# One block kernel, eight PSUM banks: the attention's output product moves from the ring of four to the bank of the down product

## What is computed

```python
sa, ca, ga, sb, cb, gb = modulation(c)            # six rows of 256 per batch
h = layernorm(x) * (1 + ca) + sa
#   attention: 16 heads of 16, causal, window 128
h1 = layer_norm(h, ln1_w, ln1_b)
q, k, v = h1 @ Wq + bq, h1 @ Wk + bk, h1 @ Wv + bv
ctx = softmax(q k^T / 4 + band) @ v
y = h + ctx @ Wo + bo
y = y + gelu(layer_norm(y) @ W1 + b1) @ W2 + b2   # W1: 256 x 1024, W2: 1024 x 256
x = x + ga * y
h = layernorm(x) * (1 + cb) + sb                  # then a second feed-forward:
xr, xk = mixes of h with its row before           # r = sigmoid(xr Wr), k = relu(xk Wk)^2
out = x + gb * (r * (k @ Wv2))
```

## Time and profile before

| | us |
|---|---|
| median of 3 runs | 619.79 |
| lowest, highest | 619.2, 621.26 |
| the profiled execution, whole | 619.02 |
| its span, first to last instruction | 617.3 |
| PE busy (matrix multiplications) | 560.3 |
| PE busy (weight loads) | 436.6 |
| DVE, ACT, POOL busy | 417.1, 446.9, 378.1 |

### The profile page before, as it was taken

How to read it: one execution, slowest core, us unless ns; L and a number is a source line. 1 busy time by engine, 2 the same in 40 slices (tenths; PEclk the granted TensorE clock), 3 DMA queues, 4 the chain that set the end, 5 groups by cost and what they waited for, 6 DMA issues and landing times.

```text
span 617.3 us, 16387 instructions
## 1 busy us (share of the span) xinstructions
PE 560.3 (91%) x6448; PEld 436.6 (71%) x6448; DVE 417.1 (68%) x830; ACT 446.9 (72%) x749; POOL 378.1 (61%) x610
## 2 busy tenths in 40 slices
PE   8798987889898998999899989899999999999996
PEld 5467765666766776677667767677777768877785
DVE  4786676794656968786967777757766484465453
ACT  2616676679868787887879686978697798956642
POOL 4277527738947357676776679575748377953330
PEclk9999988989999999999999999999999999999999
DMA  5555435413224034422334152332522134111111
GB/s 163 218 162 129 115 83 161 121 53 81 74 70 111 20 86 123 102 77 71 101 96 116 43 142 88 90 91 74 135 49 69 47 87 122 55 29 36 44 44 34
DMA packets 46363, 55.72 MB, mean 90 GB/s; under 512 B 11643, under 2 KB 33469, under 8 KB 46286
## 3 DMA queue, kind: packets, MB, share of 16 engines
q1 hardware_dynamic: 44454, 53.81, 31.8%
q10 hardware_dynamic: 1832, 0.87, 0.6%
HBM read 22.31 MB, written 4.49 MB: 43 GB/s over the span
## 4 chain that ended last, share of the span: by engine, by line
PE 54%; DVE 20%; ACT 13%; issue 6%; POOL 4%; DMA 2%; ACTq 0%; SPq 0%; DVEq 0%; POOLq 0%
DVE nmax L1853 5%; PE rest L361 4%; PE rest L486 3%; PE quad L398 3%; PE rest L447 3%; PE rest L474 3%; PE rest L498 3%; PE quad L342 3%; PE rest L449 3%; PE rest L448 3%; DVE hid_lo L1914 2%; ACT p L1151 2%; PE quad L307 2%; DVE quad L1850 2%; ACT rest L1202 2%
## 5 line engine op out<-in xcount | busy, mean ns | idle before, releaser
L2588 POOL TENSOR_SCALAR_AFFINE_SELECT p<-p 128x448 f32<-128x448 f32 x64 | 39.0, 610 | 88.1 <-ACT p L1151 63.5
L1853 DVE TENSOR_REDUCE nmax<-quad 128x8 f32<-128x1032 f32 x64 | 78.9, 1233 | 2.2
L430 PE MATMUL rest<-bt_hi,w_hi 128*128 128x256 f16 x256 | 70.2, 274 | 5.0 <-DVE hid_lo L1914 3.5
L1151 ACT ACTIVATE p<-quad,scale_s 128x576 f32<-128x576 f32 (+1 forms) x73 | 59.0, 823 | 20.0 <-PE quad L342 19.7
L1202 ACT ACTIVATE rest<-rest,bias,scale_g 128x256 f32<-128x256 f32 x128 | 62.8, 533 | 12.0 <-PE rest L432 11.5
L447 PE MATMUL rest<-w_hi,hid_hi 128*128 128x256 f16 x256 | 69.9, 273 | 1.7 <-DVE hid_lo L1914 1.7
L432 PE MATMUL rest<-bt_hi,w_lo 128*128 128x256 f16 x256 | 69.8, 273 | 0.0
L431 PE MATMUL rest<-bt_lo,w_hi 128*128 128x256 f16 x256 | 69.8, 273 | 0.0
L449 PE MATMUL rest<-w_hi,hid_lo 128*128 128x256 f16 x256 | 69.8, 272 | 0.0
L448 PE MATMUL rest<-w_lo,hid_hi 128*128 128x256 f16 x256 | 69.8, 272 | 0.0
L1914 DVE SCALAR_TENSOR_TENSOR hid_lo<-rest,inv_f,hid_hi 128x512 f16<-128x512 f32 x64 | 46.5, 740 | 29.1 <-ACT hid_hi L1212 29.1
(11 more groups left out here) (239 smaller groups left out, 1544.4 us busy)
## 6 DMA issues: line engine op xcount, KB each, us to landing
k_st<-k_two SPq DMA_DIRECT2D x64, 128.0 KB, 2.5
v_blk<-vn SPq DMA_DIRECT2D x16, 512.0 KB, 6.0
q_st<-q_two SPq DMA_DIRECT2D x64, 64.0 KB, 2.2
k_st<-k_two SPq DMA_DIRECT2D x64, 64.0 KB, 2.0
rb<-den_rows SPq DMA_DIRECT2D x16, 256.0 KB
x<-x SPq DMA_DIRECT2D x16, 256.0 KB, 3.0
out<-x SPq DMA_DIRECT2D x16, 256.0 KB, 2.2
xa<-x SPq DMA_DIRECT2D x7, 512.0 KB, 4.3
```

What stands on the lines that cost most here:

```text
L430: e.matmul(dst, w1_hi[:, k, ms], bt_hi[:, k, :], start=(k == 0), stop=False)
L1151: e.activation(p32[gp % SLOTS][:, c0:c0 + 2 * w].rearrange("p (n c) -> p n c", n=2), (rest if gp < APART else quad)[:, b0 % HQ:b0 % HQ + 2 ...
L1853: e.tensor_reduce(nmax[:, :, :, qt].rearrange("p a j -> p j a"), quad[:, :, 2 * QB - 2:2 * WIN].rearrange("p j (c a) -> p j a c", a=2), AX ...
```

## The change

The output product takes its bank from `ring_f` instead of `ring_s`; `residual_a` reads it there. Its first call also waits for the last scores that lived in this bank (s_ex), and the waits in `warm` become holds, which are issued once per semaphore and value. The order of the calls stays on every engine.

```diff
             def warm(n, times):
                 if n == 0:
                     e.wait_ge(s_pool, POOL_IDENT)
-                if n == WARM:
-                    e.wait_ge(s_peak, 10)
-                if n == WARM + 5:
-                    e.wait_ge(s_ex, 2 * APART)
+                if WARM <= n < WARM + 5:
+                    hold(e, s_peak, 10)
+                if n >= WARM + 5:
+                    hold(e, s_ex, 2 * APART)
...
-                bank, free = ring_s.take(("wo", i), s_x1, i + 1)
+                bank, free = ring_f.take(("wo", i), s_x1, i + 1)
                 if t2 == 0:
                     e.wait_ge(s_ct, 2 * (n + 1))
                 if i == 0:
                     e.wait_ge(s_wos, 1)
+                    e.wait_ge(s_ex, 2 * APART)
                 hold(e, *free)
...
-                e.tensor_tensor(x1[:, ts, :], ring_s.at["wo", i][:, :].rearrange("p (t c) -> p t c", t=2), h[n % 3][:, ts, :],
+                e.tensor_tensor(x1[:, ts, :], ring_f.at["wo", i][:, :].rearrange("p (t c) -> p t c", t=2), h[n % 3][:, ts, :],
                                 ALU.add).then_inc(s_x1, 1)
```

## The result

The changed kernel is slower: 623.32 us (median of 20 runs, 620.1 to 628.51) against 619.61 us (20 runs of the kernel before, 617.24 to 622.04). The ratio is 1.0059 with a 95% interval of 1.0043 to 1.0075, that is +3.7 us (2.7 to 4.6). The forecast was 621.4 us, +1.6; the range of 617.4 to 624.4 holds the result, and slower, which the prediction counts from +1.86 us on, had its largest chance, 0.46. The range owes that to the room left for rivals 2 and 3; the sum itself is 2.1 us short.

What follows compares the result with a forecast made beforehand. PE was taken to bound most stretches, with short spells of DVE or ACT late. Gains -1.3, half batch 2 +0.3, half batch 14 +2.1 and pairs +0.5 gave +1.6 us: 621.4 us, range 617.4 to 624.4.

Steps and rivals of the forecast that it cites:

- rival 2: ACT becomes late: its 14 extra instructions cost 3.5 instead of 0.5 us; +4.6, 624.4 us, slower; chance 0.13.
- rival 3: The clock falls at PE's new pause near 553: +2.0 on top, +3.6, 623.4 us, slower; chance 0.15.
- The new wait at half batch 14: The down product, right behind the output product, waits for its bank to be read: +2.1 us, absorbed by nothing.
- Half batch 2: The down product begun at 166.85 would wait for the output product's read ending at 167.14: +0.3 us.
- The gains: Waits taken from PE at half batches 4, 6, 7, 9 and 10: -1.3 us in sum.
- Half batch 7: A 0.43 us wait goes with nothing standing behind it: -0.43 us.
- half batches 9 and 10: At 9 a 0.37 us wait before scores goes, taken as -0.3; at 10 PE wins DVE's 0.20 us.
- Half batches 4, 6, 8 and 10: Waits before maxima and output product go, -0.6 us together, nothing at 8; the down product is not later than today.
- The pairs of scores: Shifted banks split more pairs, 14 more ACT instructions at 250 ns; net two on the chain, +0.5 us.
- the two prices in the prediction: Cost of a split pair: 250 ns from the profile rows, 187 ns by the Trainium skill.
- Rival 1: Every wait taken from PE shortens the run: -6.1 from removed waits, -3.2 us in all, 616.6 us, faster; chance 0.16.

Runs made afterwards that it cites:

- the changed kernel run again: The changed kernel as it is, measured a second time against the kernel before: 621.12 us, 1.0031.
- the three filled pauses: Small multiplications in PE's pause behind product 14: 14 in the changed kernel (622.09 us), 8 with only product 14 moved (621.61 us), 8 in the changed kernel (620.36 us).
- kernel with products 2 and 14 back: The changed kernel with output products 2 and 14 in ring_s and the ring turned on at each moved product: 619.0 us, 0.9986; second sample 618.4 us, 0.9987.
- the kernels with the old pairs: Changed kernel, ring_s turned on at each moved product so pairs keep their banks: product 14 back, 617.47 us; products 2 and 14 back, 619.0 us.
- the slope over 73: The kernel before with every pair of scores from group 12 on split, 73 more instructions on ACT: 622.37 us, 1.0045.

## Why the prediction was right or wrong, point by point

- **The new wait at half batch 14, +2.1 us.** Right: 2.18 us in three kernels, 3.84 and 3.85 where the clock fell. It was right that nothing behind it absorbs it: the difference does not change between 560 and 597 us.
- **The sum left out the clock.** This is the step that failed. The forecast's likeliest case kept full speed behind the pause, and rival 3, at 0.15, carried the fall at +2.0. It was seen in two of three profiles with the unfilled pause and cost 1.66 us; rival 3 had the size nearly right and the chance too low. The evidence used for the low chance, a window without any work of PE in which the clock stood at 1.00, does show that such a pause need not lower the clock, and the profile of the changed kernel run again shows it once more. It was no reason for a chance as low as 0.15. The rule of the Trainium skill (TensorE: Matmul & The Clock Gate, "What's actually happening"), that the clock follows how busy PE has been, agrees with the two levels seen, 1.00 and 0.50, and with the three filled pauses, behind which the clock stood at 1.00.
- **Half batch 2, +0.3 us.** Right: the difference steps by +0.34 between the 23rd and 24th read of the maxima, and not where product 2 stays.
- **The gains, -1.3 us.** The direction was right; 0.94 us were measured, and the parts were wrong. Half batch 7 was to give 0.43 because "nothing stands behind them". PE did start product 7 sooner, but three calls further on `values_b`, of the second feed-forward, then waited for DVE's L1917 of the up product, which had stood hidden behind the old wait:

```profile
PE rest L501 <- DVE hid_lo L1917: 0.5, 1, 0.5
```

  (waits of PE, kernel with products 2 and 14 back, 324 to 332 us). In the kernels with the old pairs, half batches 9 and 10 gave 0.4 each in place of 0.3 and 0.2, and 4 and 6 gave 0.1 each in place of 0.2.
- **Half batches 4, 6, 8 and 10.** The text said that the down product is not later than before, and that L447 would wait twice in the whole kernel. It waits six times: the 0.78 us before the maxima came back as 0.50 to 0.78 before the down product. The price was right all the same, since the old wait was of the same size; the count was wrong.
- **The pairs of scores, +0.5 us.** Too high: 0.2 or 0.3 us by leaving them out, 0.4 us by the slope over 73. The count of 14 was exact. The price of a split pair was not: 2 x 578 - 906 adds up durations that overlap by 0.1 us, and ACT's busy time grows by 0.14 us a pair, not 0.25. Of the two prices in the prediction the lower one, 187 ns, was nearer. The argument against rival 2 set 2.0 us of waiting before whole pairs beside 11.7 before split ones; that compares wide pieces with narrow ones, since before whole narrow pairs ACT waited 18.0 us.
- **Rival 1**, the waits going through in full: of 6.1 us, 0.9 came. At nearly every place the next wait was a few tenths away.

Added up from the traces: -0.9 + 0.3 + 0.3 + 2.2 = +1.9 us with the clock kept, +3.6 with its fall. The forecast of +1.6 is close to the first of these partly by luck: it took the gains 0.4 us too large and the pairs 0.2 too dear. The +3.7 of the first 20 runs is near the second sum, the +1.9 of the second sample is the first.

## What to carry to other kernels

A buffer taken from one ring and given to another does not remove a wait, it chooses who waits; look in the order of calls for the one place where the two users of the shared buffer stand next to each other, since here it made the whole loss. If a pause of about 2 us opens in an engine that was full, price it with and without the clock's fall behind it, and try first whether another call fits into it. For changes under 1% compare the two traces instruction by instruction, and take the difference in steps: it told 0.3 us where 12 timed runs could not.

## What was not expected of the hardware

- Where two kernels have the same instructions, their traces repeat to some 0.1 us over 300 us. What moves a whole execution is the clock in the first 140 us, where code that is the same in all kernels stood from 2.0 us early to 4.2 us late by 32 us, and now and then a transfer: L1873, which scales the context after it, came late enough in two profiles to hold product 14 for 1.2 and 1.3 us, and in two others it made a step of some 0.5 us near 494 us.
- The fall of the clock behind one pause of the same kernel is not certain: with 2.0 us of waiting it fell in both profiles, with 1.2 us and 1.5 us of waiting around the product it did not. Nor is the length of a wait enough to tell: near the start, the changed kernel run again waited 2.29 us and kept 1.00, while its first profile waited 2.85 us there and stood at 0.59 in the window behind it.

```profile
23.79 0.39 PE L267 MATMUL quad<-at_hi,wa_hi 128*128 128x512 f16 x1 [2.29 <-DVE at_lo L1827]
...
24.00:26.00 2.00, 2.00 (x11) 0.93 (x10) 0.65 (x2) 2.00 (x5) 0.00 (x0) 1.00 0.22 76
```

- 10 us of busy time added to ScalarE, which is busy for 72% of the span, lengthened the kernel by 2.2 us by the traces and 2.8 by the runs (interval 1.3 to 4.3).
